# Moving the first value products and two rope projections of a windowed attention ahead of the second half's transposes

## What is computed

```python
x = x + 0.5 * _L0_ffn_ref(_layernorm(x), gate_w, up_w, down_w, ...)
x = x + _L0_attn_ref(_layernorm(x), Wq, Wk, Wv, Wo, lam)

# _L0_attn_ref: 16 query heads, 4 key and value heads, 128 wide
q = x @ Wq;  k = x @ Wk;  v = x @ Wv
q = q * cos + rotate_half(q) * sin          # "rope"; k likewise
s1 = q1 @ k1.T / 8;  s2 = q2 @ k2.T / 8     # the two halves of each head
a1, a2 = softmax(s1), softmax(s2)           # within the window
diff = relu(a1 - lam * a2);  diff = diff / (sum(diff) + 1e-6)
out = (diff @ v) @ Wo
```

## Time and profile before

| | us |
|---|---|
| median of 3 runs | 1616.38 |
| lowest, highest | 1614.93, 1616.94 |
| the profiled execution, device time | 1616.59 |
| its span in the profile | 1614.8 |
| TensorE busy | 1409.9 (87%) |
| VectorE busy | 1199.5 (74%) |
| ScalarE busy | 1019.0 (63%) |
| granted TensorE clock, mean | 0.964 |

### The profile page before, as it was taken

One profiled execution on the slowest core, in us unless ns is written; L12 is line 12 of the kernel. 1 busy time (PEld: TensorE's weight loads), 2 busy tenths in 40 slices (PEclk: granted clock), 3 DMA queues, 4 the chain that ended last, 5 costly groups with the idle time before them and its releaser, 6 DMA issues. The chain is left out here.

```text
span 1614.8 us, 41750 instructions
## 1 busy us (share of the span) xinstructions
PE 1409.9 (87%) x15104; PEld 937.5 (58%) x15104; DVE 1199.5 (74%) x3775; ACT 1019.0 (63%) x2716; POOL 41.2 (3%) x49
## 2 busy tenths in 40 slices
PE   6888889978999878888988989988989889988888
PEld 2544555656455446556756756665666667566634
DVE  6848888974842487898888889898888988974221
ACT  5617888995611456777777777686777767754220
POOL 0000000000000000000000000000000000000000
PEclk9989899989999997999999999999999999979999
DMA  4025001000030011122121212212121211200010
GB/s 168 0 83 128 15 15 28 2 2 1 1 134 0 28 31 49 20 62 56 23 66 52 69 20 63 61 31 52 58 63 19 69 55 23 51 25 15 0 55 26
DMA packets 128489, 69.30 MB, mean 43 GB/s; under 512 B 104464, under 2 KB 115984, under 8 KB 127264
## 3 DMA queue, kind: packets, MB, share of 16 engines
q1 hardware_dynamic: 128288, 66.64, 15.3%
HBM read 51.36 MB, written 6.98 MB: 36 GB/s over the span
## 5 line engine op out<-in xcount | busy, mean ns | idle before, releaser
L1666 DVE SCALAR_TENSOR_TENSOR arena<-arena 128x1024 f32<-128x1024 f32 x144 | 183.0, 1280 | 19.6 <-ACT arena L1235 19.3
L882 PE MATMUL bank<-xt,arena 128*128 128x512 f32 x384 | 183.1, 608 | 9.6 <-ACT arena L1227 8.2
L1745 DVE TENSOR_TENSOR arena<-arena 128x512 f32<-128x512 f32 x224 | 155.2, 693 | 9.5 <-PE bank L938 4.5
L716 PE MATMUL bank<-xt,arena 128*128 128x512 f32 x320 | 142.2, 601 | 3.8 <-DVE arena L1478 3.8
L1234 ACT COPY arena<-bank 128x512 f32<-128x512 f32 x96 | 56.2, 585 | 92.4 <-PE bank L882 90.8
L882 PEld LDWEIGHTS bank<-xt,arena 128*128 128x128 f32 x384 | 68.4, 194 | 71.9 <-issue 71.6
L716 PEld LDWEIGHTS bank<-xt,arena 128*128 128x128 f32 x320 | 60.3, 192 | 85.3 <-issue 85.1
L735 PE MATMUL bank<-arena 128*128 128x256 f32 (+2 forms) x384 | 98.4, 404 | 6.2 <-DVE arena L1478 5.3
L938 PEld LDWEIGHTS bank<-arena 128*32 128x32 f32 x5120 | 59.8, 115 | 75.5 <-issue 64.4
L1164 ACT ACTIVATE arena<-arena 128x128 f32<-128x128 f32 x256 | 99.5, 393 | 0.0
L938 PE MATMUL bank<-arena 128*32 128x32 f32 x5120 | 74.7, 204 | 25.8 <-DVE arena L1747 17.3
(11 more groups left out here) (170 smaller groups left out, 3313.3 us busy)
## 6 DMA issues: line engine op xcount, KB each, us to landing
arena<-d_w SPq DMA_DIRECT2D x16, 519.0 KB, 6.4
arena<-beta_scratch SPq DMA_DIRECT2D x16, 512.0 KB, 5.7
arena<-zero_scratch SPq DMA_DIRECT2D x14, 512.0 KB, 4.6
arena<-arena SPq DMA_DIRECT2D x64, 64.0 KB, 2.6
arena<-zero_scratch SPq DMA_DIRECT2D x15, 256.0 KB, 2.9
arena<-arena SPq DMA_DIRECT2D x12, 256.0 KB, 3.8
arena<-w_scratch SPq DMA_DIRECT2D x2, 1376.0 KB, 6.1
arena<-f_idx SPq DMA_DIRECT2D x2, 1072.0 KB, 8.4
```

The lines of the kernel that those rows point to most:

```text
L716: last = pe.matmul(bank[2 * w + n % 2][0:rows, :], (WU if f < 2 else WU1R)[:, w, k, m * P:m * P + rows], XT[:, k, hf * HALF:(hf + 1) * HAL ...
L882: last = pe.matmul(bank[b][:], DW[:, par, c:c + P], XT[:, k, rhs], start=(k == 0), stop=(k == KC - 1))
L1666: dve.scalar_tensor_tensor(out=CT[:, x], in0=RAW[:, x, 3 - j:3 - j + S], scalar=DW[:, par, tap:tap + 1], in1=CT[:, x], op0=ALU.mult, op1=A ...
L1745: dve.tensor_tensor(kq, kq, left, ALU.mult)
```

## The change

TensorE: `values(0)`, `rope_project(0)`, values 1 to 3 and `rope_project(1)` now stand ahead of `ln_turn(1, 1)`; the wait at the start is for `xt_ready` 6 in place of 8, and the wait for 8 stands behind the transposes, before `rope_project(2)`. Ropes 0 and 1 write banks 0 and 1, and 2 and 3, in place of 6 and 7, so the waits for `rope_read` of the first three are gone. Values 0 and 1 wait for the feed-forward's last reads of banks 4 and 5 (`y_scaled` 3 and 4). ScalarE copies values 0 to 3 before it copies the second half's transposes. VectorE no longer waits for `xt_ready` 8. The sync engine loads the first four heads' query weights right behind the store of W1, then waits for the feed-forward's last product (`down_done` 4), then loads tables and masks.

```diff
+def rope_bank(m, a):
+    return (2 * m if m < ROPE_AHEAD else 6) + a
...
# sync engine
-                sp.wait_ge(x_ready, 4)
-                sp.wait_ge(xt_ready, 8)
...
+                for h in range(4):
+                    query_weights(h)
+                sp.wait_ge(down_done, 4)
                 for hf in range(2):
                     cs = slice(hf * HALF, (hf + 1) * HALF)
                     sp.dma_start(COS[:, cs], rope_in[0][:, cs]).then_inc(at_turns[hf], 16)
...
-                    for h in range(2 * hf, 2 * hf + 2):
-                        query_weights(h)
...
# TensorE
-                ln_turn(1, 1)
                 pe.wait_ge(at_kv_w, 144)
-                pe.wait_ge(xt_ready, 8)
+                pe.wait_ge(xt_ready, 6)
...
-                        wait(pe, rope_read, 2 * (m - 1) + a + 1 if m else 0)
+                        if m > ROPE_AHEAD:
+                            pe.wait_ge(rope_read, 2 * (m - 1) + a + 1)
...
-                            last = pe.matmul(bank[6 + a][:], w, XT[:, k, hf * HALF:(hf + 1) * HALF],
+                            last = pe.matmul(bank[rope_bank(m, a)][:], w, XT[:, k, hf * HALF:(hf + 1) * HALF],
...
                 def values(t):
-                    wait(pe, v_copied, t - 1)
+                    if t < 2:
+                        pe.wait_ge(y_scaled, 3 + t)
+                    else:
+                        pe.wait_ge(v_copied, t - 1)
...
+                values(0)
                 rope_project(0)
-                for t in range(4):
-                    if t % 2 == 0:
-                        rope_project(t // 2 + 1)
+                for t in range(1, 4):
                     values(t)
+                rope_project(1)
+                ln_turn(1, 1)
+                pe.wait_ge(xt_ready, 8)
+                rope_project(2)
...
# ScalarE
-                ln_copy(1, 1)
-                act.wait_ge(w1_saved, 16)
...
                 for t in range(4):
                     keep_values(t)
+                ln_copy(1, 1)
+                act.wait_ge(w1_saved, 16)
...
# VectorE
-                dve.wait_ge(xt_ready, 8)
                 dve.wait_ge(w1_saved, 16)
...
-                        last = dve.tensor_tensor(to, bank[6 + a][:], table[:, cs], ALU.mult)
+                        last = dve.tensor_tensor(to, bank[rope_bank(m, a)][:], table[:, cs], ALU.mult)
```

## The result

| | before | changed |
|---|---|---|
| median of 16 runs, us | 1616.46 | 1605.66 |
| lowest, highest | 1608.22, 1622.42 | 1594.04, 1615.57 |
| profiled execution, device time | 1616.59 | 1604.80 |
| its span | 1614.8 | 1603.0 |
| `scores(0)` starts at | 117.46 | 106.04 |

The ratio is 0.9933, 95% interval 0.9914 to 0.9951: 10.8 us less, 7.9 to 13.9 by the interval. The forecast was 1607.0 in 1604.5 to 1611.0, faster with 0.93. Single runs scatter much more than the three shown before the prediction: those lay within 2 us, the sixteen within 14 and 22.

What follows compares the result with a forecast made beforehand. TensorE's stream was taken to bound the kernel between 89 and 117, 5.93 us of it empty. Terms 13.72, 1.76 and 3.43 put `scores(0)` at 108.0, 9.45 us earlier: 1607.0 us, range 1604.5 to 1611.

Steps and rivals of the forecast that it cites:

- Values and two ropes: TensorE after `ffn_down`: values 0 to 3 and ropes 0 and 1, 32 records at 3.43 us per eight, 13.72 us.
- Transposes and copies: TensorE before rope 2: second half's transposes, two copies and start of next product, 1.76 us at full clock, 0.73 idle.
- Rope 2: TensorE's last step before `scores(0)`: eight records, 3.43 us, putting `scores(0)` at 108.0.
- VectorE: Rope 0 starts at 95.8, rope 1's sums end at 105.4, 2.6 us ahead of `scores(0)`.
- Loads: SP's queue: eight query weights issue in 4.2 to 6.9 us; tables land 93.2 to 95.7, turned keys by 104.0.
- the reserve of 1.5 + 2.6 us: Late tables would first use VectorE's 1.5 us gap between ropes 0 and 1, then its 2.6 us lead over `scores(0)`.
- Nothing at a fixed time behind the seam: Loop and after: no step found that starts at a fixed time, so the 9.45 us carries to the end.
- a loop that takes over 2 us longer: Sign of being wrong: the attention loop, first step to last, taking longer than before by more than 2 us.
- split by cause: The 9.45 us at the seam: 5.94 from filling the idle stretch, 0.98 from transposes, 2.53 from rope 0's slow records.
- Rival 2: No change: something else releases `scores(0)`, such as VectorE behind late tables; 1616.4 or within 3 us; chance 0.04.
- Rival 3: Slower: low clock holds through the moved stretch, `scores(0)` at 126, total 1625; chance 0.03.
- Rival 1: Smaller gain: clock falls once more, at rope 2 or in the loop; 1609.5 to 1613; chance 0.12.

Runs made afterwards that it cites:

- `tables_late`: Changed kernel with tables and masks loaded only after the second half's copies, as before; seam 27.95 us, ratio 0.9973 to the kernel before.
- `values_only`: Changed kernel with all four values ahead of the transposes and all ropes behind them; seam 18.71 us, ratio 0.9917 to the kernel before.
- the clock alone: Kernel before with 24 products nobody reads filling TensorE's idle stretch ahead of the transposes, no work moved; seam 27.24 us, ratio 1.0017.
- the loads alone: Kernel before with only the sooner loads of query weights and tables; seam 28.40 us, ratio 0.9991.
- `early_turn`: Changed kernel with transposes right behind values 1, ahead of values 2, 3 and rope 1; seam 18.17 us, ratio 0.9917; repeat 18.16 us, 0.994.
- `same_banks`: Changed kernel with ropes 0 and 1 in banks 6 and 7 as before, with the waits this takes; seam 20.77 us, ratio 0.9922.
- `early_turn_warm`: Kernel with transposes right behind values 1, plus 11 unread products ahead of the first feed-forward's last `ffn_down`; seam 18.17 us, ratio 0.9942 to the kernel before.

## Why the prediction was right

It was right in its number, and at the seam in its mechanism, where its sum holds term by term. That the time behind the seam would stay as it was is not borne out in the same way (last point below). Times are from the end of `ffn_down`.

- *Values and two ropes, 13.72 us.* Measured 100.65 - 86.89 = 13.76. No wait on bank or copy shows among them. One reading was off: 97.7 and 99.4, given as the starts of values 2 and 3, are their ends in the sum's own terms. The spare time ahead of values 3 was thus forecast as 2.8 us and is 1.1 by the sum, still enough.
- *Transposes and copies, 1.76.* Measured 102.41 - 100.65 = 1.76, 0.72 of it idle, the same as the row it was taken from the earlier trace rows.
- *Rope 2, 3.43.* Measured 106.04 - 102.41 = 3.63. Half of the 0.2 is that it starts after a wait (3.70 us long, not 3.60); the other half is the step from the last product to `scores(0)`, which was there before too: 117.46 - 113.93 = 3.53. The 0.2 are nearly all of the difference between 9.45 and 9.21.
- *VectorE.* Rope 0 at 6.7 forecast, 93.49 - 86.89 = 6.60 measured; last sum at 16.3 and 16.57. The lead over `scores(0)` is 2.6 as worked out.
- *Loads.* Eight query weights in 4.41 us (4.2 to 6.9 forecast); the tables without any wait of VectorE. `tables_late` tests the reserve of 1.5 + 2.6 us that the prediction gave late tables: VectorE's rope 0 started 12.85 us later than in the changed kernel, so `scores(0)` should lose 8.75 us, and it lost 8.80. What ended last there were the turned keys, which have a reserve of their own: in `tables_late` and `values_only` `scores(0)` starts 4.66 and 4.65 us after their first issue, so in the changed kernel they were there by 101.9, 4.1 us early (forecast 104.0 against 108.0).
- *Nothing at a fixed time behind the seam.* No step at a fixed time shows, but the agreement of 1497.34 and 1496.97 us is luck. The prediction put a loop that takes over 2 us longer down as a sign of being wrong. It took 1.27 us longer in the first profile and 2.98 in the second. VectorE's busy time in the loop was 198.85 us before, and 199.05 and 198.92 in the two; TensorE's was 205.78, and 207.50 and 209.19. So the time was lost on TensorE.

The total is less exact than the seam. The measured 1605.66 lies 1.3 us under the forecast, and its interval, 1602.6 to 1608.5, reaches below the range's 1604.5; that the median fell inside is in part luck.

What did not hold is the split by cause. I wrote 5.94 us for the idle stretch and 3.5 for the low clock as though each could be had by itself, and gave the loads no share. The runs show parts that need each other: the clock alone 1.1, the loads alone 0.0, both 3.2; the order of TensorE with late tables 0.4, and with the loads 9.2. The sum was right because it followed the new order from start to end with every engine in it; the split took a difference of TensorE's rows apart without asking who would be late next in each partial kernel.

Rival 2 (the tables release `scores(0)`) did not come, but `tables_late` shows that its mechanism is real, at a place where it costs 8.8 us. Rival 3 (low clock through the moved stretch) did not come: the clock is 1.00 over six banks as over four. The Trainium skill describes a pattern in "TensorE: Matmul & The Clock Gate", section "A second HAM failure mode: psum-queue depth-cycling", which the page saw with bf16 products of 512 columns. With the fp32 products here it shows in no profile of this seam: the low clock came only behind a single long wait (5.93 us before, 8.73 in `tables_late`). Rival 1 is there, in the loop. In the changed kernel's first profile two projections of the pair loop took longer than the usual 3.60 us:

```profile
154.15 4.32 PE L771 MATMUL bank<-xt,arena 128*128 128x512 f32 x8
...
168.85 5.49 PE L771 MATMUL bank<-xt,arena 128*128 128x512 f32 x8
```

Before, one such projection took 5.34. So these were 1.7 us over 3.60 before and 2.6 now; in the second profile they were 5.97 and 4.63, 3.4 over. The loops of the two profiles of `early_turn` and the one of `same_banks` took 237.2 to 237.3 us, no longer than before; that of `values_only` took 240.65. Whether the changed kernel's loop starts in a state that brings the further spell, or two profiles happened to have it, is open; no run tests that.

## What to carry to other kernels

When an engine idles for data, ask for work behind it in its stream that needs none of that data. Its amount has to fill the gap, and which work it is mattered little at this seam (values alone did as well as values and ropes, in one profile). Then follow what that work needs on the other engines' queues: here the loads stood behind the same wait, and without moving them too, at least 8.8 of 9.2 us would have been lost. Put behind a step whose result is copied something that does not read the copy.

Price a set of edits as one new order, and do not read the parts of the sum as what each edit would bring alone.

## What was not expected of the hardware

The same code takes visibly different times. The 48 records of `ffn_down` behind a 2.67 us idle stretch took 12.00 us in eight of the eleven profiles that have this stretch, 13.4 in two and 16.62 in one. From 75.00 to 89.10 us the mean granted clock was 1.00 in the changed kernel's 12.00, 0.88 in both profiles with 13.4, and 0.64 in the one with 16.62. What follows `scores(0)`, the same work in all twelve profiles, took from 1493.67 us (`same_banks`) to 1508.8 (`early_turn_warm`). Over the sixteen runs of the changed kernel mean granted clock and time go together (correlation -0.83): 0.978 with 1594.04 us, 0.962 with 1615.57. That the clock makes most of this scatter is the likely reading, not shown by an edit. A change of 9 us stands out of that scatter only in the median of many runs, and one of 1 us was only seen in the profile's stretches.
